# An attentive GRU step on one core: attention scores computed in two layouts, the exponential written already turned, and reset and candidate joined in a scan

## The reference

```python
def step(h, x_t):
    hid = jnp.broadcast_to(h[:, None, :], (Bn, Sn, Hn))
    combined = jnp.concatenate([hid, enc_hiddens], axis=2)
    score = jnp.tanh(jnp.einsum('bsk,kh->bsh', combined, W_att))
    score = jnp.einsum('bsh,h->bs', score, V_att[:, 0])
    attn = jax.nn.softmax(score, axis=-1)
    context = jnp.einsum('bs,bsh->bh', attn, enc_hiddens)
    inp = jnp.concatenate([x_t, context], axis=1)
    gz, gr, gh = jnp.split(inp @ Wi + b, 3, axis=1)
    rz, rr, rh = jnp.split(h @ Uh, 3, axis=1)
    z = jax.nn.sigmoid(gz + rz)
    r = jax.nn.sigmoid(gr + rr)
    hh = jnp.tanh(gh + r * rh)
...
_, outs = jax.lax.scan(step, last_hidden, jnp.swapaxes(dec_seq, 0, 1))
```

## Time and profile before

| what | value |
|---|---|
| median of three executions | 5413.7 us |
| the profiled execution, span | 5413.8 us |
| first and last attnT copy of the loop | 426.4 and 1931.8 us |
| PE busy over the span | 4614.7 us (85%) |
| DVE busy over the span | 2884.4 us (53%) |
| ACT busy over the span | 2082.3 us (38%) |

### The profile page before, as it was taken

The page is one execution under the profiler, slowest core; times in us unless marked ns, Lnnn a source line. Parts: engine busy times, 40 slices in busy tenths (PEclk is TensorE's granted clock), DMA queues, the critical chain, the costliest instruction groups (busy, mean ns, idle before and its releaser), DMA issues. The chain is left out here.

```text
span 5413.8 us, 111310 instructions
## 1 busy us (share of the span) xinstructions
PE 4614.7 (85%) x45206; PEld 3112.5 (57%) x45501; DVE 2884.4 (53%) x9511; ACT 2082.3 (38%) x4120; POOL 576.5 (11%) x1302
## 2 busy tenths in 40 slices
PE   5489999999999965889989889899778979788784
PEld 3357777777777753555555555555444756566463
DVE  6634555555555535777766677666455224433433
ACT  2223333333333312665665666566433322212221
POOL 3300111111111112111111111111000000000000
PEclk8789999999999976999999999999889989878786
DMA  0000000000000011000000000000010010000000
GB/s 26 23 18 2 2 2 2 2 2 2 2 2 2 2 61 54 4 4 6 7 6 4 4 9 4 6 1 1 1 40 1 1 44 1 1 1 1 1 1 9
DMA packets 32272, 49.22 MB, mean 9 GB/s; under 512 B 8244, under 2 KB 23638, under 8 KB 31136
## 3 DMA queue, kind: packets, MB, share of 16 engines
q1 hardware_dynamic: 28448, 38.27, 2.2%
q10 hardware_dynamic: 2304, 2.11, 0.1%
q0 software_dynamic: 1024, 1.78, 0.1%
HBM read 37.72 MB, written 4.19 MB: 8 GB/s over the span
## 5 line engine op out<-in xcount | busy, mean ns | idle before, releaser
L2299 DVE TENSOR_REDUCE l_m<-psum 128x2 bf16<-128x512 f32 x768 | 503.8, 692 | 148.8 <-PE psum L1904 146.5
L2175 ACT ACTIVATE l_probs<-psum,l_mcol 128x1024 f32<-128x1024 f32 x384 | 406.3, 1109 | 159.2 <-PE psum L1942 159.2
L1184 PE MATMUL psum<-g_gx,ident 128*128 128x128 f32 x1536 | 416.0, 389 | 18.0
L1173 PE MATMUL psum<-g_still,ident_bf 128*128 128x256 bf16 (+3 forms) x1551 | 391.5, 281 | 1.7 <-PEq L58 1.7
L1904 PE MATMUL psum<-l_kb,l_qmb 32*128 32x256 bf16 x1536 | 295.4, 273 | 56.1 <-DVE l_m L2299 52.4
L1252 ACT ACTIVATE g_th<-g_pre 128x256 f32<-128x256 f32 x512 | 191.7, 417 | 314.3 <-DVE g_pre L1285 314.3
L1184 PEld LDWEIGHTS psum<-g_gx,ident 128*128 128x128 f32 x1536 | 279.4, 195 | 12.8
L1942 PE MATMUL psum<-l_qm,l_keys 32*128 32x256 f32 x3072 | 265.1, 418 | 13.3 <-issue 13.3
L2186 ACT COPY l_heads_out<-psum 128x256 f32<-128x256 f32 (+1 forms) x292 | 130.0, 445 | 369.8 <-PE psum L1968 186.3
L1285 DVE TENSOR_TENSOR g_pre<-g_encp,psum 128x256 f32<-128x256 f32 x512 | 192.8, 418 | 132.9 <-PE psum L1202 122.4
L2299 DVE TENSOR_REDUCE l_cm<-psum 128x4 bf16<-128x256 f32 x400 | 166.0, 427 | 179.8 <-PE psum L1904 179.6
(11 more groups left out here) (567 smaller groups left out, 9761.9 us busy)
## 6 DMA issues: line engine op xcount, KB each, us to landing
s_w<-in_S_w SPq DMA_DIRECT2D x16, 256.0 KB, 5.0
f_w<-in_F_w SPq DMA_DIRECT2D x2, 2048.0 KB, 12.5
l_wf<-in_L_W SPq DMA_DIRECT2D x6, 576.0 KB, 3.8
l_w<-in_L_W SPq DMA_DIRECT2D x1, 3072.0 KB, 10.6
l_nw<-in_L_nw SPq DMA_DIRECT2D x1, 2304.0 KB, 8.0
l_wc<-in_L_W SPq DMA_DIRECT2D x6, 384.0 KB, 3.0
h_w<-in_H_W ACTq DMA_DIRECT2D x16, 129.0 KB, 3.0
h_w<-in_H_W SPq DMA_DIRECT2D x16, 129.0 KB, 3.0
```

What stands on the lines that cost most here:

```text
L1173: pe.matmul(psum[:, bank, 0:cols], cst["ident_bf"][:], still[:, 0:cols], start=True, stop=True)
L1184: pe.matmul(psum[:, bank, 0:P], cst["ident"][:], repeated(gx(gate, s)), start=True, stop=False)
L2175: act.activation(probs[:, u % 2, chunk, :].rearrange("p (g n) -> p g n", g=GROUP), psum[:, 0:GROUP, S * chunk:S * chunk + S], ACT.Exp, bia ...
L2299: dve.tensor_reduce(place, psum[:, c.bank(("max", u, g)), 0:x.tiles * x.width] .rearrange("p (t k) -> p t k", t=x.tiles), AX.X, ALU.min)\
```

## The change

The loop body is rewritten and the hardware loop around it is gone.

- Scores are computed twice: as before (`score_rows`), and with `th` stationary, 64 columns wide, and the score vector moving, repeated to 16 columns (`score_cols`), which puts keys on partitions in bank 2, every eighth column. A product `apart` first fills bank 2 with 0 or -1e30, and a last one adds the minimum (rounded to bfloat16, broadcast as stationary operand). ScalarE's exponential of bank 2 is `attnT` itself; the old turning product and the copy are gone. A second exponential, after it on ScalarE, gives only the sum, through its accumulator.
- The candidate's input and state product share bank 6, interleaved: the input GXC holds a zero beside each value and is added with `paired`. `reset` holds a zero beside each tanh r, and one `tensor_tensor_scan` makes 0.5·(1 + tanh r) times the state product plus the rest, in the place of two VectorE instructions.
- The contexts come in the order r, z, h. ScalarE copies r and z, VectorE h.
- `input_part` of gate z moves from the start of the next step to the end of this one, behind that of gate r. The state products of gates r and z move from behind the scores to before them.
- `keep_busy` goes from seven products a step (2112 columns) to four (1088 columns).

```diff
+        GX, GXC = sb("gx", [P, 2, B, S]), sb("gxc", [P, B, S, 2])
+        reset, u = sb("reset", [P, B, 2]), sb("u", [P, B, 2])
...
+                pool.memset(GXC[:], 0.0).then_inc(sig["shares_cleared"], 1)
...
+                    dst = GX[:, i, 2 * p:2 * p + 2, :] if i < 2 else GXC[:, 2 * p:2 * p + 2, :, 1]
...
+                def input_part(gate, bank, s):
+                    pe.matmul(psum[:, bank, 0:P], cst["ident"][:], repeated(GX[:, gate, :, s]), start=True, stop=False)
+
+                def paired(cols):
+                    return cols.unsqueeze(1).to_broadcast([P, REPEATS // 2, B, 2])
+
+                def score_rows(i):
+                    for p in range(PAIRS):
+                        last = pe.matmul(psum[32 * p:32 * p + 32, 1, 0:C], vneg[:, i, :], th[:, i, p, :],
+                                         start=i == 0, stop=i == 1)
+                    return last
+
+                def score_cols(i, pairs):
+                    for p in pairs:
+                        pe.matmul(psum[HALVES[i], 2, 2 * p + i:P:B], th[:, i, p, :], vcol[:].to_broadcast([P, REPEATS]),
+                                  start=False, stop=False)
+
...
+                        pe.wait_ge(sig["candidate_input_ready"], s)
+                    pe.matmul(psum[:, 6, 0:P], cst["ident"][:], paired(GXC[:, :, s, :]), start=True, stop=False)
+                    if s:
+                        pe.wait_ge(sig["state_ready"], s)
+                    pe.matmul(psum[:, 6, 0:P], uh_half[:], paired(hs.unsqueeze(2).to_broadcast([P, B, 2])), start=False, stop=False)
+                    pe.matmul(psum[:, 5, 0:P], uh[:, 1, :], repeated(hs), start=False, stop=False)
+                    pe.matmul(psum[:, 4, 0:P], uh[:, 0, :], repeated(hs), start=False, stop=False)
+                    pe.matmul(psum[:, 2, 0:P], cst["ident_bf"][:],
+                              apart[:].rearrange("p q i -> p (q i)").unsqueeze(1).to_broadcast([P, REPEATS, B]), start=True, stop=False)
+                    pe.wait_ge(sig["tanh_ready"], 2 * s + 1)
+                    score_rows(0)
+                    score_cols(0, (0, 1))
+                    pe.wait_ge(sig["tanh_ready"], 2 * s + 2)
+                    score_rows(1).then_inc(sig["scores_ready"], 1)
+                    score_cols(0, (2, 3))
+                    score_cols(1, range(PAIRS))
+                    pe.wait_ge(sig["smin_ready"], s + 1)
+                    pe.matmul(psum[:, 2, 0:B], smin_bf[:].to_broadcast([P, P]), pick_bf[:], start=False, stop=True)\
+                        .then_inc(sig["shifted_ready"], 1)
+                    keep_busy(0, 320, 2)
+                    pe.wait_ge(sig["attnT_ready"], s + 1)
+                    context_part(1, 3, "context_r_ready")
+                    context_part(0, 2, "context_z_ready")
+                    context_part(2, 7, "context_h_ready")
+                    keep_busy(0, 320)
+                    pe.wait_ge(sig["shares_ready"], s + 1)
+                    pe.wait_ge(sig["context_r_taken"], s + 1)
+                    turn_part(0, psum[:, 5, 0:B], "gate_r_ready")
...
+                    if s + 1 < S:
+                        pe.wait_ge(sig["tanh_r_ready"], s + 1)
+                        input_part(1, 5, s + 1)
+                        pe.wait_ge(sig["tanh_z_ready"], s + 1)
+                        input_part(0, 4, s + 1)
+                        keep_busy(3, 128)
...
+                    act.wait_ge(sig["shifted_ready"], s + 1)
+                    act.activation(attnT[:, 0:B], psum[:, 2, 0:B], ACT.Exp).then_inc(sig["attnT_ready"], 1)
+                    act.wait_ge(sig["smin_wide_ready"], s + 1)
+                    act.activation(attn[:], psum[:, 1, 0:C], ACT.Exp, bias=smin[:], scale=-1.0, accum_out=ssum[:])\
+                        .then_inc(sig["sum_ready"], 1)
...
+                    dve.wait_ge(sig["scores_ready"], s + 1)
+                    dve.tensor_reduce(smin_bf[:], psum[:, 1, 0:C], AX.X, ALU.min).then_inc(sig["smin_ready"], 1)
+                    dve.wait_ge(sig["smin_ready"], s + 1)
+                    dve.tensor_copy(smin[:], smin_bf[:]).then_inc(sig["smin_wide_ready"], 1)
...
+                    dve.tensor_tensor_scan(u[:].rearrange("p b two -> p (b two)"), reset[:].rearrange("p b two -> p (b two)"),
+                                           candidate.rearrange("p b two -> p (b two)"), 0.0, ALU.mult, ALU.add)\
+                        .then_inc(sig["candidate_input_ready"], 1)
```

More of the change, by code:

```diff
@@ L1023, in _ @@
                 residual(B - 1)
-STEPS_A_PASS = 256
+REPEATS = 16
 def attentive_gru(nc, dram, X, psum, cst):
@@ L1049, in attentive_gru @@
         z, zT = sb("z", [P, TILES, D]), sb("zT", [P, TILES * P])
-        GX = sb("gx", [P, 3, B, S])
+        GX, GXC = sb("gx", [P, 2, B, S]), sb("gxc", [P, B, S, 2])
         HT = sb("ht", [P, B, S])
@@ L1053, in attentive_gru @@
         h = sb("h", [P, 2, B])
+        uh_half = sb("uh_half", [P, D])
         pre, th = sb("pre", [P, 2, PAIRS, C]), sb("th", [P, 2, PAIRS, C])
         smin, ssum, inverse = sb("smin", [P, 1]), sb("ssum", [P, 1]), sb("inverse", [P, 1])
+        smin_bf, pick_bf, apart = sb("smin_bf", [P, 1], BF16), sb("pick_bf", [P, B], BF16), sb("apart", [P, PAIRS, 2], BF16)
         attn, attnT, shares = sb("attn", [P, C]), sb("attnT", [P, B + 32]), sb("shares", [P, B])
@@ L1058, in attentive_gru @@
         wa_half = sb("wa_half", [P, D])
-        kept, tr, tz, u, u2, cand, omz, zh, part = (sb(n, [P, B]) for n in ("kept", "tr", "tz", "u", "u2", "cand", "omz", "zh", "part"))
+        kept, tz, cand, omz, zh, part = (sb(n, [P, B]) for n in ("kept", "tz", "cand", "omz", "zh", "part"))
+        reset, u = sb("reset", [P, B, 2]), sb("u", [P, B, 2])
         still = sb("still", [P, 512], BF16)
@@ L1115, in gates @@
                     act.wait_ge(sig["gates_ready"], n + 1)
-                    act.activation(GX[:, i, 2 * p:2 * p + 2, :], psum[:, 2 + n % 6, :].rearrange("p (b s) -> p b s", b=2),
+                    dst = GX[:, i, 2 * p:2 * p + 2, :] if i < 2 else GXC[:, 2 * p:2 * p + 2, :, 1]
+                    if n == 2:
+                        act.wait_ge(sig["shares_cleared"], 1)
+                    act.activation(dst, psum[:, 2 + n % 6, :].rearrange("p (b s) -> p b s", b=2),
                                    ACT.Identity, bias=bias[:, i:i + 1]).then_inc(sig["gates_taken"], 1)
@@ L1139, in _ @@
                 dve.memset(still[:], 0.0)
+                dve.memset(reset[:], 0.0)
+                dve.memset(apart[HALVES[0], :, 0:1], 0.0)
+                dve.memset(apart[HALVES[0], :, 1:2], NEG)
+                dve.memset(apart[HALVES[1], :, 0:1], NEG)
+                dve.memset(apart[HALVES[1], :, 1:2], 0.0)
                 steps.after(dve.memset(vneg[:], 0.0))
@@ L1142, in _ @@
                 dve.tensor_scalar(wa_half[:], wa[:, 0, :], 0.5, None, ALU.mult)
+                dve.tensor_scalar(uh_half[:], uh[:, 2, :], 0.5, None, ALU.mult)
                 dve.tensor_tensor(pick8[:], pick[:, 0, :], pick[:, 1, :], ALU.add)
+                dve.tensor_tensor(pick_bf[:], pick[:, 0, :], pick[:, 1, :], ALU.add)
                 for i in range(2):
```

226 lines of the change are left out of this document (86 added, 140 removed).

## The result

| what | before | after |
|---|---|---|
| median, 20 runs each | 5409.3 us (5396.32 to 5429.03) | 5426.18 us (5414.1 to 5443.64) |
| ratio | | 1.0033, 95% interval 1.0021 to 1.0045 |
| span of the profiled execution | 5413.8 us | 5435.8 us |

The changed kernel is slower: by 16.9 us between the medians, by 0.33% in the ratio, whose interval leaves out 1. The forecast was 5473 us, 59 us more than before. The sign is right and the time lies in the outer range (5345 to 5557), but the loss is less than a third of the one forecast. It falls short of the forecast's own range (5440 to 5510), and into the class of under 0.5% that the prediction calls "same" and gave 0.13.

The account below looks back on a forecast made before the run. The prediction saw a chain in which each engine waits for the one before, TensorE close behind. Per step 5.90 - 0.05 + 0.28 = 6.13 us, +0.23; times 256, +59: 5473 us, own range 5440 to 5510, outer range 5345 to 5557.

Parts of the forecast that it names:

- same: Whole kernel: the class of outcomes within 0.5% of the time before, given a chance of 0.13.
- first half: Step from query result to the contexts' first load, 2.98 us before: forecast to change by -0.05, ends -0.46 and +0.28.
- first rival: TensorE's first part of the step: columns serial and GXC at half rate, 6.46 a step, 5557 us; chance 0.16.
- second half: Step from contexts' load to next query result, 2.92 us before: forecast +0.28, as inputs r and z both stand here.
- The second: TensorE's score products: shape changes free and columns hidden, 5.72 a step, 5368 us, faster; chance 0.17.
- The third: Input products: doubled record comes from the loop's register address and goes with the loop, 5.75 a step, 5375 us; chance 0.13.
- The fourth: Whole step: both parts cancel, contexts 0.2 to 0.35 early as some shape changes overlap, 5.9 a step; chance 0.13.
- The fifth: TensorE's clock falls with 1024 idle columns a step fewer: some 2 us a step, +500 us; chance 0.03.

Follow-up runs that it names:

- e1_contig: Changed kernel with GX stored so that the 8 values of one position lie side by side: 5381.93 us, ratio 0.9929 to the kernel before.
- e2_rows_first: Changed kernel with all score columns behind the second half of the score rows, array halves in turn: 5355.06 us, ratio 0.9892 to the kernel before.
- e7_two_scans: Changed kernel with a second scan in each step, into a buffer nobody reads: 5430.02 us, ratio 1.0015 to the kernel before.
- e6_before_contig: Kernel before the change, with only GX stored with neighbours side by side, loop and register address kept: 5402.94 us, ratio 0.9967.
- e4_no_idle: Changed kernel without any of its four idle products a step: 5649.75 us, ratio 1.0429 to the kernel before.
- e11_no_columns: The joined kernel with score columns undone, exponential, turn and copy as before the change, plus an idle product: 5405.62 us, ratio 0.998 to the kernel before.
- joined kernel: Changed kernel with GX neighbours stored side by side and all score columns behind both score rows: 5313.26 us, ratio 0.9805 to the kernel before.

## Why the prediction was right in its sign and wrong in its size

**What held.** The changed TensorE order decides: `e1_contig` and `e2_rows_first` won what their waits had shown, `e7_two_scans` nothing. In the first half, measured from the query result, forecast in brackets: first rows 0.98 (0.97), first columns 1.23 (1.225), second rows 1.56 (1.555), other columns 1.81 (1.81), minimum 1.95 (1.94). The drain of 0.10 at a change from 32 to 64 columns, taken from other shapes, is there: with the prediction's 0.22 for a narrow record the rows' last one starts at 3.51 + 0.32 - 0.22 = 3.61 and streams 0.05, so to 3.66, and the columns' load comes at 3.76. For the change back only the sum of columns and change is read, 0.33 as forecast. That a change of tiling mode drains the engine is the rule of the Trainium skill (TensorEngine Tiling (Array Packing), Key Properties), and the trace agrees. The columns of both halves ran side by side, so the first rival fell. GXC's second record starts at 2.38 + 0.47 - 0.27 = 2.58 and the next product at 2.69: 0.11, not 0.22. Its first record stands 0.20 before the second; L1206 in the kernel before, whose operand is contiguous, shows 0.49 - 0.27 = 0.22 there (at 1002.19), so that is not the layout's. The Trainium skill (SBUF — State Buffer, Specifications) states lines of 16 bytes with two hits wanted for full bandwidth; for pairs that gave the 0.11, and the trace agrees. In the second half tanh r came at 1.30 (1.30), and `part` waited for TensorE: forecast to end 0.3 early, by the trace it ends 0.21 ahead of the load (1.92 to 2.13, of which a prompt release takes 0.05). It has less to spare because it ends 2.52 after the contexts' load, not 2.39. Shares (6.08) were hidden by 0.16 (0.15). The scan lasted 0.19 (0.20).

**What failed are terms of the sum, not its mechanism.** The forecast step was +0.23 (-0.05 and +0.28), the measured one +0.065 (by halves -0.14 and +0.21). The difference of 0.165 lies in three mis-sized terms: the minimum's product in the first half, the start of the inputs and the last query product in the second.

1. First half, 2.84 instead of 2.93. I priced the product with the minimum at 0.28 from load to result, from the float32 product at L1187 (0.43 for its two records, less 0.11 for the second and 0.04 for ScalarE's start). A single bfloat16 record gave its result at about 5.10, 0.18 after its load at 4.92: -0.10. A row of the same type was at hand: L1173's bfloat16 record lasts 0.27, of which 0.11 streams 256 columns, so by estimate 0.16 and a little for 8 columns. The load came 0.03 late, and the 0.02 added for doubt about GXC was not needed: -0.09 in all.
2. Second half, 3.13 instead of 3.20. I used a wait of 0.11 between tanh r and the input's load, as at 6.71 to 6.82; it is 0.06 here (6.85 to 6.91), and with the first record 0.03 behind its load the inputs start at 1.57 instead of 1.70. The way from there to L1226 gives that back, with 1.27 (0.97 to 2.24) where the sum has 1.13: the first gap of the inputs is 0.27, and the idle product and zh's records take longer too. L1226 starts at 2.84 (2.83). There its second record starts 0.03 behind the first, not 0.11 (0.29 for two records, of which one lasts 0.26): -0.08. Its load had come 0.11 before it, under zh's product. Where `part` arrives last, as in `e1_contig`, load and first record start together, and the two records are 0.39 - 0.26 = 0.13 apart. The sum's 0.37 for the pair also went against its own row, since L1202 lasts 0.32, the figure that the prediction itself uses for the query results at 2.22 and 8.12.

Each is small; times 256 steps they are 42 us, more than the whole measured effect. That the sign came out right was in part luck: the error was 0.165, and one of 0.23 would have turned it.

**The rivals.** The second (5368 us, 5.72 a step) fell, since shape changes cost what was said; but `e2_rows_first` shows that its period can be had by order (5.691). The third fell with `e6_before_contig`, and its figure of 5.75 for a full-rate input is near the 5.809 that `e1_contig` measured. The fourth, both halves cancelling to within 0.5%, is what came out, though not for its reason: the contexts are 0.14 earlier, not 0.2 to 0.35, and no shape changes overlap. The fifth did not happen. The ground against it, that TensorE is fuller, is true of the records (200 of 200 us against 195) but says nothing of the clock: `e4_no_idle` is nearly as full by the records as the kernel before (191 of 200 us) and runs at 0.81, while `e11_no_columns` holds 1.00:

```profile
1100.00:1300.00 200.00, 184.02 (x2420) 139.69 (x2420) 84.51 (x409) 71.90 (x274) 21.36 (x102) 1.00 0.01 2
```

Its price, 2 us a step, was for a clock that stays down; at a mean of 0.81 the measured one is 0.935.

## What to carry to other kernels

When an engine is close behind the chain, place its work by which wait it stands behind: the same columns gained 0.335 us a step behind both score rows, and, by 0.335 - 0.278 and not by a run of its own, only 0.06 with four of them between the rows. Read the gap between records of equal products with different operands; a strided moving operand cost 0.11 a record and went with one change of layout. And for a sum of 0.01 us terms times 256 steps, take the time from a product's load to its result from one of the same type and number of records, or widen the range.

## What was not expected of the hardware

- Removing 1088 idle bfloat16 columns a step lowered the granted clock to 0.81 and cost 0.935 us a step, though TensorE's records still filled 96% of the time. In the joined kernel, removing 448 or 640 of them cost nothing, and removing all cost 0.091.
- Sixteen 64-wide column records (eight products), alternating between the two halves of the array, take the time of twelve, four in one half and then eight in the other: 0.55 in weight loads.
- Their output columns lie every eighth in a bank, and their loads still follow each other at 0.55 / 16 = 0.034 us over both halves. With 16 columns a record the loads set this pace, so it does not price such outputs as such.
- A scan over 16 elements on VectorE takes 0.19 us, against 0.17 for an elementwise instruction over 8.
